# A two-layer cross-attention and feed-forward kernel on one core: from block 3 on the queries are made from raw x, turned in memory, with centred weights and the deviations multiplied in behind the product, and the drain and the end go by chunk pairs

## What is computed

```python
x = x + L0_xattn(layernorm(x), ctx)   # 16 heads of 16, 64 keys; then relu(out @ W1 + b1) @ W2 + b2
x = x + L0_ffn(layernorm(x))          # 8 experts' LoRA (rank 16) on one wi (256 -> 1024), relu, wo; top 2 gates
x = x + L1_xattn(layernorm(x), ctx)   # one head of 256, 64 keys
x = x + L1_ffn(layernorm(x))          # linear 256 -> 256
# in L0_xattn:  q = layernorm(x) @ Wq + bq,   layernorm(x) = (x - m) / sqrt(v + eps), no gain, no shift
```

## Time and profile before

| what | value |
|---|---|
| time, median of 3 runs | 326.35 us (326.2 to 326.74) |
| profiled execution, its own time | 326.24 us |
| its span, first to last instruction | 324.1 us |
| mean granted TensorE clock | 0.994 |
| TensorE busy in the span | 310.8 us (96%) |
| VectorE / ScalarE / GpSimd busy | 231.7 / 173.3 / 146.2 us |

### The profile page before, as it was taken

The page is one execution under the profiler, slowest core; times in us unless marked ns, Lnnn a source line. Parts: engine busy times, 40 slices in busy tenths (PEclk is TensorE's granted clock), DMA queues, the critical chain, the costliest instruction groups (busy, mean ns, idle before and its releaser), DMA issues.

```text
span 324.1 us, 6486 instructions
## 1 busy us (share of the span) xinstructions
PE 310.8 (96%) x2497; PEld 285.6 (88%) x2497; DVE 231.7 (71%) x644; ACT 173.3 (53%) x355; POOL 146.2 (45%) x150
## 2 busy tenths in 40 slices
PE   8979998999999999999999999999999999999982
PEld 6758896899989998999989998999899989999771
DVE  3856675846987777957895689577886779456766
ACT  4357655582575358465657267535844574434511
POOL 1664772635053814563173607280538144703431
PEclk9999999999999999999999999999999999999997
DMA  7589930003100320013100400032002200000000
GB/s 256 162 227 351 194 88 2 0 17 85 32 1 2 73 92 0 2 42 90 36 0 16 116 34 0 2 89 76 2 0 58 73 3 1 2 26 9 0 34 32
DMA packets 14702, 18.85 MB, mean 58 GB/s; under 512 B 2224, under 2 KB 11312, under 8 KB 14416
## 3 DMA queue, kind: packets, MB, share of 16 engines
q1 hardware_dynamic: 12640, 14.99, 17.6%
q10 hardware_dynamic: 2032, 3.44, 3.1%
HBM read 9.51 MB, written 2.62 MB: 37 GB/s over the span
## 4 chain that ended last, share of the span: by engine, by line
PE 85%; DVE 5%; ACT 3%; DMA 2%; SPq 2%; POOL 2%; issue 1%; DVEq 0%; POOLq 0%; ACTq 0%
PE psI L302 14%; PE psI L458 13%; PE psP L311 12%; PE psI L311 11%; PE psS L311 7%; PE psT L302 4%; PE psP L393 3%; PE psT L326 3%; PE psS L379 3%; PE psP L394 2%; PE psT L525 2%; PE psS L356 2%; PE psI L620 1%; PE psP L612 1%; PE psP L434 1%; DMA xin<-in_x 1%
## 5 line engine op out<-in xcount | busy, mean ns | idle before, releaser
L1445 POOL TENSOR_TENSOR rs<-ve,mhalf 128x2 f32<-128x2 f32 x30 | 22.5, 749 | 93.4 <-DVE ve L1068 93.4
L1464 POOL TENSOR_TENSOR hid_l<-r,hid_h 128x512 fp32r<-128x512 f32 x32 | 40.9, 1293 | 17.0 <-ACT hid_h L858 17.0
L1147 DVE SCALAR_TENSOR_TENSOR r<-psI,nbi,r 128x256 f32<-128x256 f32 x60 | 26.1, 478 | 22.3 <-PE psI L458 22.3
L1458 POOL TENSOR_TENSOR hs_l<-hs,hs_h 128x512 fp32r<-128x512 f32 x16 | 20.9, 1307 | 42.1 <-ACT hs_h L838 42.0
L458 PE MATMUL psI<-at_h,lb_h 128*128 128x256 f32 x120 | 35.4, 295 | 1.5 <-DVE at_l L1139 1.5
L853 ACT ACTIVATE r<-psI,first 128x256 f32<-128x256 f32 x60 | 25.1, 476 | 17.8 <-PE psI L458 17.7
L458 PE MATMUL psI<-at_l,lb_h 128*128 128x256 f32 x120 | 33.8, 282 | 0.0
L458 PE MATMUL psI<-at_h,lb_l 128*128 128x256 f32 x120 | 33.7, 281 | 0.0
L1088 DVE RECIPROCAL rec<-psP 128x256 f32<-128x256 f32 x16 | 28.0, 1753 | 2.6 <-PE psP L394 2.6
L800 ACT ACTIVATE xn<-xmid,nmr,rs 128x256 f32<-128x256 f32 x16 | 8.7, 594 | 37.1 <-POOL nmr L1449 37.1
L822 ACT ACTIVATE ex<-psS 128x512 f32<-128x512 f32 x32 | 18.3, 599 | 18.3 <-PE psS L379 18.2
(11 more groups left out here) (258 smaller groups left out, 862.7 us busy)
## 6 DMA issues: line engine op xcount, KB each, us to landing
stack<-qu_h SPq DMA_DIRECT2D x60, 64.0 KB, 2.0
xin<-in_x SPq DMA_DIRECT2D x8, 256.0 KB, 2.8
stack<-qu_l SPq DMA_DIRECT2D x30, 64.0 KB, 2.0
out<-x ACTq DMA_DIRECT2D x7, 256.0 KB, 2.0
raw_wi<-in_wi SPq DMA_DIRECT2D x1, 1024.0 KB, 8.6
raw_wo<-in_wo SPq DMA_DIRECT2D x1, 1024.0 KB, 11.9
kv<-in_kv SPq DMA_DIRECT2D x2, 384.0 KB, 8.8
raw_w<-in_w ACTq DMA_DIRECT2D x1, 512.0 KB, 7.7
```

The source lines that it names most:

```text
L1147: last = V.scalar_tensor_tensor(out=R1[:, f, :], in0=bank[:, k * T:(k + 1) * T], scalar=nbi[:, f:f + 1], in1=R1[:, f, :], op0=MAX, op1=ADD)
L1445: G_.tensor_tensor(rs[:, :], ve[:, :], mhalf[:, :], ALU.pow).then_inc(S(f"ln{j}_rs"), 1)
L1458: G_.tensor_tensor(HS[1][:, two, :], HS32[:, two, :], as32(HS[0][:, two, :]), ALU.subtract).then_inc(S("hsl"), 1)
L1464: G_.tensor_tensor(HL[:, two, :], R1[:, two, :], as32(HH[:, two, :]), ALU.subtract).then_inc(S("hidl"), 1)
```

## The change

- **Queries of blocks 3 to 7** (`TURNED = 3`). The host passes x a second time with features on the partitions (`in_xt`). SyncE loads it (`load_xt`) into `xn1`; ScalarE copies its high part (`across_high`), GpSimd takes the low part. TensorE no longer transposes for these blocks, ScalarE no longer normalises them, VectorE's `low(1, h)` and GpSimd's -m rs fall away.
- **The deviations.** SyncE's `across(h)` writes rs (128 x 2) to memory and reads it back as `scales`, one row of 256 on all partitions. VectorE's `queries_scaled(h)` multiplies the product by it into `qs`, in two halves; ScalarE's `queries` and VectorE's `queries_low` read `qs` instead of the bank.
- **The centred weights**, once. At the start TensorE takes the column means (`query_means`, in the place of three fillers) and VectorE copies them; in body 1 GpSimd makes the centred weights (`query_weights`, two instructions of 128 x 512) between `attended_low` and `hidden_low`, ScalarE writes their high part (`centred_high`) and VectorE their low part (`centred_low`, ahead of `row_max(2, 0)`).
- **Order in the body**: ScalarE's `hidden_high(a, 1)` now stands ahead of `queries(h)`, the wait for `z` moves down to `transposes(2, a)`.
- **Drain**: TensorE starts `f_second(7, 0)` and `(7, 1)` ahead of `c_attend`; VectorE sums the hidden layer ahead of `third_residual`; the last residual of block 6 moves from VectorE to two instructions of GpSimd; its store moves into `end`. `last_f_out` goes by pairs of chunks.
- **End**: VectorE takes `residual(1)` ahead of the statistics of tile 0; ScalarE copies both linear parts ahead of the softmax.

```diff
+TURNED = 3
@@ sync
                 if b > 0:
-                    sp.wait_ge(S("ln1_xh"), b * NT)
+                    if b <= TURNED:
+                        sp.wait_ge(S("ln1_xh"), b * NT)
+                    else:
+                        sp.wait_ge(S("ln1_st"), b * NT)
                     sp.wait_ge(S("xres"), b)
...
+            def load_xt(b):
+                if b == TURNED:
+                    sp.wait_ge(S("ln1_T"), b)
+                else:
+                    sp.wait_ge(S("ln1_l"), b)
+                sp.dma_start(xn1[:, :], io["xt"][b * P:(b + 1) * P, :]).then_inc(S("xt_in"), 16)
+
+            def across(b):
+                n = b - TURNED
+                sp.wait_ge(S("ln1_rs"), b + 1)
+                if n > 0:
+                    sp.wait_ge(S("q32"), n * KC)
+                sp.dma_start(dr_scales.rearrange("(p t) -> p t", p=P), lnst[1][4][:, :]).then_inc(S("scales_out"), 16)
+                sp.wait_ge(S("scales_out"), (n + 1) * 16)
+                sp.dma_start(scales[:, :], dr_scales.unsqueeze(0).broadcast_to([P, T])).then_inc(S("scales_in"), 16)
...
                     load_x(b)
+                if b >= TURNED:
+                    load_xt(b)
+                    across(b)
                 stack_q(b, 0)
@@ tensor
+            def query_means():
+                pe.wait_ge(S("consts"), 1)
+                parts = [as32(t["wq"][:, c * D:(c + 1) * D]) for t in (wh, wl) for c in range(KC)]
+                for n, part in enumerate(parts):
+                    last = mm(I_(1)[:, 0:D], avg[:, 0:1].broadcast_to([P, P]), part, start=n == 0,
+                              stop=n == len(parts) - 1)
+                last.then_inc(S("centred"), 1)
...
             def last_f_out(b):
-                for a, c, signal in ((0, 0, "hidh"), (0, 1, None), (1, 0, "hidl")):
-                    for t in range(NT):
-                        for f in range(NFF):
...
+                def high(t, u):
+                    pe.wait_ge(S("hidh"), b * NDF + u + 1)
+                    for c in range(2):
+                        for f in (2 * u, 2 * u + 1):
+                            mm(P_(t)[:, 0:D], HH[:, f, t * P:(t + 1) * P], (WH, WL)[c]["wo"][:, f, :],
+                               start=c == 0 and f == 0, stop=False, skip_group_check=True)
...
+                high(0, 0)
+                high(0, 1)
+                high(0, 2)
+                high(1, 0)
+                high(0, 3)
+                high(1, 1)
+                high(1, 2)
+                low(0)
+                high(1, 3)
+                low(1)
@@ tensor, drain
                 f_first(f, 1, BANKS[1])
+                f_base(f, 3, BANKS[3])
                 c_transpose(c)
-                f_base(f, 3, BANKS[3])
                 f_first(f, 2, BANKS[2])
+                f_second(f, 0, BANKS[0])
                 f_first(f, 3, BANKS[3])
+                f_second(f, 1, BANKS[1])
                 c_attend(c)
-                for u in range(NDF):
-                    f_second(f, u, BANKS[u])
+                f_second(f, 2, BANKS[2])
+                f_second(f, 3, BANKS[3])
                 last_f_out(f)
@@ tensor, body
                     a_hidden(a, 0)
-                if H_ and a > 0:
-                    if f == 0:
-                        pe.wait_ge(S("gw"), 1)
-                    if C_:
-                        pe.wait_ge(S("z"), (c + 1) * NT)
+                if f == 0:
+                    pe.wait_ge(S("gw"), 1)
                     transposes(1, h, T_(1))
...
+                if C_:
+                    pe.wait_ge(S("z"), (c + 1) * NT)
                 if A_:
                     transposes(2, a, T_(1))
@@ scalar
+            def across_high(b):
+                act.wait_ge(S("xt_in"), (b - TURNED + 1) * 16)
+                act.wait_ge(S("q_ps"), b)
+                A(XTA[0], XT, ACT.Identity).then_inc(S("ln1_h"), 1)
+
+            def centred_high():
+                act.wait_ge(S("q_ps"), TURNED)
+                act.wait_ge(S("centred"), 4)
+                A(wh["wq"][:, :], qs[:, :], ACT.Identity).then_inc(S("centred"), 1)
...
             def queries(b):
-                act.wait_ge(S("q_ps"), b + 1)
                 for m in range(KC):
-                    A(QU[0][:, m, :], P_(0)[:, m * T:(m + 1) * T], ACT.Identity,
-                      bias=cols[:, BQ + m:BQ + m + 1]).then_inc(S("qh"), 1)
+                    if b < TURNED:
+                        act.wait_ge(S("q_ps"), b + 1)
+                        src = P_(0)[:, m * T:(m + 1) * T]
+                    else:
+                        act.wait_ge(S("q32"), (b - TURNED) * KC + m + 1)
+                        src = Q32[:, m, :]
+                    A(QU[0][:, m, :], src, ACT.Identity, bias=cols[:, BQ + m:BQ + m + 1]).then_inc(S("qh"), 1)
@@ scalar, end
+                store(b - 1)
+                linear_part(0)
+                linear_part(1)
+                weights(0)
+                turned(0)
+                weights(1)
+                turned(1)
@@ vector
+            def queries_scaled(b):
+                n = b - TURNED
+                dve.wait_ge(S("q_ps"), b + 1)
+                dve.wait_ge(S("scales_in"), (n + 1) * 16)
+                for m in range(KC):
+                    V.tensor_tensor(Q32[:, m, :].rearrange("p (t n) -> p t n", t=NT),
+                                    P_(0)[:, m * T:(m + 1) * T].rearrange("p (t n) -> p t n", t=NT), SCALES,
+                                    MULT).then_inc(S("q32"), 1)
+
+            def centred_low():
+                dve.wait_ge(S("centred"), 5)
+                V.tensor_tensor(wl["wq"][:, :], qs[:, :], as32(wh["wq"][:, :]), SUB).then_inc(S("centred"), 1)
...
-                    V.scalar_tensor_tensor(out=QU[1][:, m, :], in0=P_(0)[:, m * T:(m + 1) * T],
+                    V.scalar_tensor_tensor(out=QU[1][:, m, :],
+                                           in0=P_(0)[:, m * T:(m + 1) * T] if b < TURNED else Q32[:, m, :],
                                            scalar=cols[:, BQ + m:BQ + m + 1], in1=as32(QU[0][:, m, :]),
                                            op0=ADD, op1=SUB).then_inc(S("ql"), 1)
@@ vector, drain
-                third_residual(c)
                 for u in range(NDF):
                     hidden_sum(f, u, BANKS[u])
+                third_residual(c)
                 scaled_linear(c)
                 dve.wait_ge(S("x3"), (c + 1) * NT)
                 norm_stats(4, c, X3)
-                fourth_residual(c)
@@ vector, end
                 residual(0)
-                statistics(0)
                 residual(1)
                 tile_low(3, b, 0, XTC)
+                statistics(0)
+                tile_low(3, b, 1, XTC)
                 statistics(1)
-                tile_low(3, b, 1, XTC)
@@ gpsimd
+            def query_weights():
+                pool.wait_ge(S("lo_w"), 1)
+                pool.wait_ge(S("centred"), 2)
+                G_.tensor_tensor(qs[:, :], as32(wh["wq"][:, :]), as32(wl["wq"][:, :]), ALU.add).then_inc(S("centred"), 1)
+                pool.wait_ge(S("centred"), 3)
+                G_.tensor_tensor(r3(qs, KC), r3(qs, KC), wqm[:, :].unsqueeze(1).broadcast_to([P, KC, D]),
+                                 ALU.subtract).then_inc(S("centred"), 1)
...
+                if a == TURNED - 2:
+                    query_weights()
+                if H_ and h >= TURNED:
+                    pool.wait_ge(S("ln1_h"), h + 1)
+                    G_.tensor_tensor(XTA[1], XT, as32(XTA[0]), ALU.subtract).then_inc(S("ln1_l"), 1)
@@ gpsimd, drain
                 scale(4, c)
+                pool.wait_ge(S("ln4_rs"), c + 1)
+                pool.wait_ge(S("z"), (c + 1) * NT)
+                pool.wait_ge(S("stored"), c * 16)
+                G_.tensor_tensor(X4, YB[c // BPB], lnst[4][4][:, :].unsqueeze(2).broadcast_to([P, NT, D]),
+                                 ALU.mult).then_inc(S("x4_in"), 1)
+                pool.wait_ge(S("x4_in"), 1)
+                pool.wait_ge(S("x3"), (c + 1) * NT)
+                G_.tensor_tensor(x4[:, :], x4[:, :], x3[:, :], ALU.add).then_inc(S("x4"), 1)
```

More of the change, by code:

```diff
@@ L148, in build @@
     gb = sb("gb", [P, BATCH * KEYS])
+    scales = sb("scales", [P, T])
+    qs = sb("qs", [P, KC * T])
+    wqm = sb("wqm", [P, D])
     xin, xr, xmid, xg, xn1 = (sb(n, [P, NT * D]) for n in ("xin", "xr", "xmid", "xg", "xn1"))
@@ L153, in build @@
     XTA = pair("xta", KC, KC * T)
+    XT, Q32 = r3(xn1, KC), r3(qs, KC)
+    SCALES = scales[:, :].rearrange("p (n t) -> p t n", t=NT)
     QU = pair("qu", KC, KC * T)
@@ L605, in last_f_out, with low @@
             def last_f_out(b):
-                for a, c, signal in ((0, 0, "hidh"), (0, 1, None), (1, 0, "hidl")):
-                    for t in range(NT):
-                        for f in range(NFF):
[L610 to L616, removed]
+                def high(t, u):
[4 more added lines that the diff above has]
+                               start=c == 0 and f == 0, stop=False, skip_group_check=True)
+                def low(t):
```

(28 more changed lines are left out.)

34 lines of the change are left out of this document (22 added, 12 removed).

## The result

| what | before | after |
|---|---|---|
| time, median of 5 runs each, side by side | 326.74 us (326.2 to 328.25) | 324.26 us (323.79 to 325.03) |
| profiled execution, its own time | 326.24 us | 324.14 us |
| its span | 324.1 us | 322.1 us |
| mean granted TensorE clock | 0.994 | 0.989 |

The ratio is 0.9929, with a 95% interval from 0.9903 to 0.9954: faster by 0.7%. The forecast was 323.8 us and the range 322.8 to 326.2. The two profiled executions differ by 2.10 us where 2.55 was forecast, so the sign and the range held, and 0.45 us of the sum are to be found.

The account below looks back on a forecast made before the run. The prediction took TensorE, busy throughout five bodies, to bound the kernel; -2.2 + 0.5 - 0.85 = -2.55 us took 326.24 to 323.7 us profiled, 323.8 as a median. Range: 322.8 to 326.2 us.

Parts of the forecast that it names:

- body 1: `centred_low` on VectorE waits for GpSimd's `hid_l`, making `first_residual` late once: +0.5 us, bounds 0.1 and 0.5 + 1.27.
- last_f_out: Last output layer on TensorE: waits for high parts mostly go, ending 1.3 to 1.4 us earlier, in 5.7 to 5.9 us.
- The transposes: Four transposes of 0.44 us leave TensorE in each of bodies 2 to 6, nothing replacing them: -2.2 us.
- The longer way to the row scores: VectorE scales the queries before ScalarE's high part, finishing 0.1 us ahead of the need: cost 0.
- the bound from above: If reading every second scale halved VectorE's scaling speed: 0.45 us a body lost, 2.2 us in all.
- Rival 2: The scaling makes the row scores wait, 0.45 us a body: 326.0 us, no change; chance 0.10.
- VectorE's queue: Instructions behind `queries_scaled` start earlier, and 0.5 us of slack is left ahead of `first_residual`: cost 0.
- rival 1: GpSimd blocks `queries_low` on VectorE in every turned body, 0.77 us lost each: 327.7 us; chance 0.10.
- The scales through memory: The scales' round trip through memory and the second load of x are covered: even 5.3 + 5.9 us fits, cost 0.
- rival 5: The turned x or the scales come late, 1 us a body: 328.8 us; chance 0.04.
- Drain and end: After the last body, output matmuls finish earlier and the end gives part back: -0.85 us, bounds -1.4 and 0.
- Rival 3: The end gives everything back, through GpSimd's residual holding ScalarE or VectorE's order: 324.65 us; chance 0.13.

Follow-up runs that it names:

- e1: Changed kernel with `last_f_out`, drain and end of the kernel before, so the turned queries alone: 324.97 us, ratio 0.9931 to the kernel before.
- e3: Changed kernel plus one filler (two unread matmuls) ahead of `a_hidden(a, 1)` in the turned bodies, where the transposes stood: 326.24 us, ratio 0.9989.
- e5: Changed kernel plus one GpSimd sum of two 128 x 512 on-chip tiles behind the second `hs_l` in the turned bodies, result unused: 326.23 us, ratio 0.9974.
- e2: Kernel before with only the new drain and end put in: 325.78 us, ratio 0.997 to the kernel before.
- e6: Changed kernel plus one GpSimd memset of 128 x 512, without input, behind the second `hs_l` in the turned bodies: 324.37 us, ratio 0.9927.
- e7: Changed kernel plus a filler ahead of each of the two transposes of the softmax weights in the end: 323.85 us, ratio 0.9909.
- e4: Changed kernel with tile 0's low output pass ahead of the second layernorm's transposes, in all bodies with an expert block: 323.68 us, ratio 0.9895.
- e8: Changed kernel with tile 0's low pass first except in body 1, two end fillers, ScalarE's second linear part behind the second exponential: 322.83 us, ratio 0.9883.

## Why the prediction was right, and where its sum was off

Four terms of the sum were off, and they partly cancel: body 1 was taken 0.4 us too dear, while the wait at the row scores (0.3), `last_f_out` (0.24) and what the end gives back (0.12) were taken too cheap, and the store's 0.27 us was scatter. That the total came within 0.5 us owes something to this luck; the main term did not.

**The transposes.** "5 x 0.44 = 2.2 us. Nothing replaces them on TensorE." Right, by e1 and by e3, which puts 0.42 us back and loses it.

**The longer way to the row scores.** "That is 0.1 us ahead of the need. [...] Cost taken: 0." This term was mis-sized: it costs 0.06 us a body, 0.3 in all. The durations of the new instructions in the changed kernel, by tile (ns: min/median/max):

```profile
L1170 DVE TENSOR_TENSOR qs<-psP,scales x10: 411/419/425, 105.6 to 242.8; 128x256 f32<-128x256 f32 x10
L884 ACT ACTIVATE qu_h<-qs,first x10: 493/501/512, 106.0 to 243.3; 128x256 fp32r<-128x256 f32 x10
```

VectorE's halves were sized right at 0.42 us, and the scales read at every second element cost nothing. So the bound from above, 0.45 us a body, is excluded. ScalarE's were not: I took 0.42 us from `oa_h`, which has no bias, and with the bias they took 0.50. Its pair of 0.91 us started at 140.25 and ends at 141.16, and the weight load followed at 141.22. From VectorE's start at 139.80 that is 1.42 us, where I had 1.22: 0.07 us are the longer second half, 0.07 its late start (at 140.67, behind ScalarE's own first half, where VectorE's second was done at 140.55), and 0.06 the step from its end to the weight load, which I had left out. No run varies the bias alone. Rival 2 was this mechanism at seven times its size. What I held against it, "TensorE is 0.44 us early, which is what makes the slack", was wrong, as e3 shows.

**VectorE's queue and rival 1.** The race was as close as walked. After, GpSimd and VectorE in body 3:

```profile
138.51 2.73 POOL L1568 TENSOR_TENSOR hs_l<-hs,hs_h 128x512 fp32r<-128x512 f32 x2 [3.12 <-ACT hs_h L911]
...
141.19 0.70 POOL L1555 TENSOR_TENSOR rs<-ve,mhalf 128x2 f32<-128x2 f32 x1
141.31 0.87 DVE L1181 SCALAR_TENSOR_TENSOR qu_l<-qs,first,qu_h 128x256 fp32r<-128x256 f32 x2
141.86 2.71 POOL L1574 TENSOR_TENSOR hid_l<-r,hid_h 128x512 fp32r<-128x512 f32 x2
...
143.88 0.69 DVE L1201 TENSOR_TENSOR xmid<-psP,xr 128x512 f32<-128x512 f32 x1 [0.57 <-PE psP L341]
```

`queries_low` starts 0.07 us behind the end of `hs_l` (141.24) and its second half goes out ahead of `hid_l`; between the two stands only rs, which didn't slow it (all ten halves took 0.47 to 0.48 us). It is GpSimd that waited, with 2.71 us for the 2.55 of the earlier trace rows. The slack of 0.57 us stayed. e5 gives the price of losing: 0.32 us a body, and not the 0.77 of the rival, because the wait was 0.99 us instead of 1.27 and the slack 0.64 instead of 0.5 (the idle 0.57 and the 0.07 by which one VectorE instruction starts ahead of the end of the last).

**Body 1.** "+0.5 us." Mis-sized: 0.10. The collision came, as these rows of VectorE and GpSimd show, and was small:

```profile
72.74 2.99 POOL L1574 TENSOR_TENSOR hid_l<-r,hid_h 128x512 fp32r<-128x512 f32 x2 [0.23 <-ACT hid_h L931]
...
73.80 0.79 DVE L1176 TENSOR_TENSOR wq_l<-qs,wq_h 128x512 fp32r<-128x512 f32 x1
...
75.64 0.67 DVE L1201 TENSOR_TENSOR xmid<-psP,xr 128x512 f32<-128x512 f32 x1
```

I had `hid_l` at 72.9; it started at 72.74, so its first instruction was over at about 74.0, and `centred_low` took 0.79 us, 0.10 more than its like. It went between GpSimd's two instructions, which took 2.99 us together for 2.54 before. I had also added the full length of each VectorE instruction, where the next one starts some 0.08 us ahead of the end. `first_residual` came at 75.64 for 75.50.

**The scales through memory.** Right with a wide cover. DMA issues after (size of one, median us to landing):

```profile
dr_scales<-rs SPq DMA_DIRECT2D x5, 1.0 KB, 3.0
scales<-dr_scales SPq DMA_DIRECT2D x5, 128.0 KB, 4.0
xn<-in_xt SPq DMA_DIRECT2D x5, 256.0 KB, 2.8
```

In body 3 rs is done at 126.9, so the scales are there at about 134 and wanted at 139.8. The round trip costs 7 us where I took up to 11.2, and rival 5 had no ground.

**Drain and end.** "-0.85 us", from "1.3 to 1.4 us earlier" and a part given back. Measured -0.49 to VectorE's last instruction. Two terms were off. `last_f_out` took 5.99 us and not 5.8, with a wait of 0.18 at the third pair. The walk through the end's order was right to 0.1 us: I had the transpose of tile 1's weights 5.2 us behind, it came 5.14 behind. And the granted clock was not in the sum at all: 0.21 us in this profiled execution, by e2, e6 and e7, which ran the same multiplications at the full clock. e6, with the same drain and end as the changed kernel, shows that it is a matter of the execution. Rival 3 would have had the end give everything back; it gave 0.62 of 1.11 us. ScalarE's store held nothing: GpSimd's residual ended at 310.0.

## What to carry to other kernels

When work is taken from the bound engine, ask of each wait behind it whether the removed work stood between the start of the waiting chain and its need: only then does its slack change. Size a new instruction by one with the same engine, source and extra operands, because here ScalarE's half with a bias took 0.08 us more than the one without, and count the steps between engines: together they were the wait. And read the granted clock in the end of a kernel in more than one execution, before a difference there is put down to the change: here slower matmuls took 0.2 us in some profiles and not in others with the same code.

## What the runs showed of the hardware that I had not expected

- **The clock's fall moved by microseconds with the same code.** Counted from the end of `last_f_out`, the granted clock fell after 5.9 us in the changed kernel (at 314.8), 5.8 in e4, 5.7 in e5, 7.5 in e3 and 7.9 in e2 and e6, all with the same drain and end; the first three hit the last multiplications, the others fell behind them. With the fillers it was 9.8 and 9.7 (e7, e8), with the old drain and end 8.4 (before) and 7.3 (e1). With one profile of each, what sets the place in a given execution stays open.
- **A blocked VectorE instruction loses less than the blocker's rest.** In e5 GpSimd's instruction had 1.18 us left when `queries_low` started, and the two halves lost 0.99. In body 1 of the changed kernel some 0.2 us were left, and `centred_low` lost 0.10.
- **Reading every second element was free.** VectorE's multiplication with the scales so read took 0.419 us, the plain one of line 1090 0.424.
- **A small write to memory took as long as a large read.** 1 KB of rs landed after 3.0 us, 256 KB of x after 2.8.
